# First gate maxima kept one step sooner, one semaphore group for the mLSTM stage, and the feed-forward's first sixteen products in the heads' tail

## What is computed

```python
x = x + tanh(g_xattn[0]) * mlstm(layernorm(x), ctx, ctx, gates, ln_scale)      # 8 heads of 32
x = x + tanh(g_ffn[0])   * ffn(layernorm(x))      # 8-bit weights + rank-16 side path, 256 -> 1024 -> 256
x = x + tanh(g_xattn[1]) * attention(layernorm(x), ctx)                        # 16 heads of 16
x = x + tanh(g_ffn[1])   * experts(layernorm(x))  # 8 routed experts, top 2, and 2 shared
# in mlstm, per head: cs = cumsum(log_sigmoid(f)); m[s] = max over t <= s of (i[t] - cs[t]) (plus cs[s])
#   C = (q k^T / sqrt(32)) * exp(a[t] - m[s]), masked;  h = C v / max(|sum C|, exp(-max)); then layernorm
# in ffn: h = gelu(W z + b + 2 B (A z)), the same form for the way down
```

## Time and profile before

| | |
|---|---|
| median of 3 runs | 1222.02 us (1220.18 to 1222.48) |
| profiled execution | 1218.74 us |
| its span | 1217.1 us |
| mean granted TensorE clock | 0.954 |
| busy: PE, DVE, ACT, POOL | 1117.4, 885.1, 702.3, 420.2 us |

### The profile page before, as it was taken

The page is one execution under the profiler, slowest core; times in us unless marked ns, Lnnn a source line. Parts: engine busy times, 40 slices in busy tenths (PEclk is TensorE's granted clock), DMA queues, the critical chain, the costliest instruction groups (busy, mean ns, idle before and its releaser), DMA issues. The chain is left out here.

```text
span 1217.1 us, 28139 instructions
## 1 busy us (share of the span) xinstructions
PE 1117.4 (92%) x9260; PEld 946.3 (78%) x9261; DVE 885.1 (73%) x2032; ACT 702.3 (58%) x1585; POOL 420.2 (35%) x559
## 2 busy tenths in 40 slices
PE   4869997999998899999998889879999999998997
PEld 1336665888887677777776489869999999998997
DVE  5858996766676788888888377467766776764666
ACT  1378995556572566667666543346755555554543
POOL 1237895531212011111120026663222232223664
PEclk9879999999998899999999878889999999999999
DMA  9246651000005455354453047656455555544664
GB/s 320 79 167 237 226 193 54 1 0 0 0 0 113 98 119 116 87 108 107 89 107 56 2 169 266 219 203 239 166 167 169 165 161 166 164 139 157 190 206 150
DMA packets 97574, 163.51 MB, mean 134 GB/s; under 512 B 12048, under 2 KB 72228, under 8 KB 95172
## 3 DMA queue, kind: packets, MB, share of 16 engines
q1 hardware_dynamic: 87652, 135.05, 38.1%
q0 software_dynamic: 9104, 26.49, 6.2%
q10 hardware_dynamic: 720, 0.71, 0.2%
HBM read 102.47 MB, written 33.69 MB: 112 GB/s over the span
## 5 line engine op out<-in xcount | busy, mean ns | idle before, releaser
L1796 DVE TENSOR_REDUCE c_mx<-d_bank 128x2 f32<-128x512 f32 x256 | 164.4, 686 | 16.5 <-PE d_bank L1948 16.1
L1711 ACT ACTIVATE c_probs<-c_t 128x512 f32<-128x512 f32 x248 | 134.7, 598 | 26.8 <-PE c_t L1974 25.9
L2929 ACT ACTIVATE d_g_full<-d_bank,d_e_bias 128x256 f32<-128x256 f32 x156 | 77.8, 498 | 105.3 <-PE d_bank L34 105.3
L32 PE MATMUL d_bank<-de_zt_hi,d_e_hi 128*128 128x256 f32 x312 | 91.0, 292 | 0.1
L34 PE MATMUL d_bank<-d_w_hi,d_g_lo 128*128 x312 | 87.8, 281 | 0.0
L33 PE MATMUL d_bank<-de_zt_lo,d_e_hi 128*128 128x256 f32 x312 | 87.8, 281 | 0.0
L33 PE MATMUL d_bank<-d_w_lo,d_g_hi 128*128 x312 | 87.8, 281 | 0.0
L32 PE MATMUL d_bank<-d_w_hi,d_g_hi 128*128 x312 | 87.8, 281 | 0.0
L34 PE MATMUL d_bank<-de_zt_hi,d_e_lo 128*128 128x256 f32 x312 | 87.3, 280 | 0.0
L3089 POOL DMA_INDIRECT d_w_lo<-d_y_rows,d_pos x64 | 65.4, 1021 | 53.3 <-ACT d_g_hi L3102 20.6
L1644 POOL CAST c_ct_hi<-c_c_raw 128x512 fp32r<-128x512 f32 x15 | 9.2, 610 | 212.3 <-PE c_misc L34 212.3
(11 more groups left out here) (433 smaller groups left out, 3849.0 us busy)
## 6 DMA issues: line engine op xcount, KB each, us to landing
d_e_raw<-in_w SPq DMA_DIRECT2D x39, 514.0 KB, 3.7
a_mb<-a_maxima SPq DMA_DIRECT2D x16, 1024.0 KB, 7.5
d_w_hi<-d_zt_kept SPq DMA_DIRECT2D x26, 512.0 KB
d_y_rows<-de_ys SPq DMA_DIRECT2D x39, 256.0 KB, 2.1
d_z_in<-d_z_rows POOLq DMA_DIRECT2D x37, 256.0 KB, 4.4
c_kt<-c_k_hi SPq DMA_DIRECT2D x64, 128.0 KB, 3.1
c_qt<-c_q_hi SPq DMA_DIRECT2D x64, 128.0 KB, 3.8
d_zt_kept<-d_w_hi SPq DMA_DIRECT2D x20, 256.0 KB
```

The costliest lines, as they stand in the source:

```text
L32: tensor.matmul(out, lhs_hi, rhs_hi, start=start, stop=False)
L1711: act.activation(probs[h % PR][:], t_bank(n, p, k), ACT.Exp).then_inc(exp_done, 1)
L1796: dve.tensor_reduce(mx[n % 2][:, :, k, p:p + 1], s_ps[h % SB], AX.X, ALU.max).then_inc(max_done, 1)
L2929: act.activation(g_full[:, m, :], hid[m][:, 0:TOK], ACT.Gelu, bias=bias[u][:, m:m + 1]).then_inc(gelu_full, 1)
```

## The change

It has three parts.

1. `rows.keep_maxima(sync, 0)` stands before the placing of the rows of step 6 instead of behind it.
2. The groups `ar_` and `ah_` are gone: `FirstInputs`, `GateRows` and the heads draw from one group `a_`, made ahead of the gates. After the heads one group is cleared, with one barrier, in place of three. The heads' tile `hz` becomes `rows.gates`, which holds `f` and `gate_i`.
3. The four PSUM banks `qk` of the heads and `hid` and `turned` of the feed-forward become one tensor, `lora.banks`, and `low` a tile that lives through both. `lower(0)` and the twelve products of `base(0, 0..2)` run at the end of the heads, behind `turn_outputs`, and so do the ACT and DVE halves of the split of `low`. PE waits for its own last product there. In the feed-forward, PE starts with the three `raised` products, and ACT with a GELU on one column (`primed`), which puts the table load ahead.

```diff
@@ mlstm_gates, sync
             for n in range(STEPS):
                 if n + KR < STEPS:
                     load_kt(n + KR)
+                if n == PLACED - 1:
+                    rows.keep_maxima(sync, 0)
                 if n < PLACED:
                     sync.wait_ge(rows_done, n + 1)
                     place_rows(sync, n)
-            rows.keep_maxima(sync, 0)
             sync.wait_ge(rows.m_kept[0], 16)
             first.load_maxima(sync)
@@ phase_mlstm
-        first = FirstInputs(nc, ctx, ctx_in, ctx_t, ln_scale, lora.ln_s, m_dram)
-        rows = GateRows(nc, ctx, tok_all, ident, m_dram)
+        sem = cleared_semaphores(nc, ctx, "a_")
+        first = FirstInputs(nc, ctx, sem, ctx_in, ctx_t, ln_scale, lora.ln_s, m_dram)
+        rows = GateRows(nc, ctx, sem, tok_all, ident, m_dram)
@@ LoraWeights.hold_zt
+        self.low = ctx.enter_context(nc.sbuf_tensor("b_low", [P, 4 * P], F32R, side="right"))
+        self.banks = self.ctx.enter_context(nc.psum_tensor("b_banks", [P, self.BANKS, 512], F32))
@@ mlstm_heads
-        sem = cleared_semaphores(nc, ctx, "a_")
-        hz = sb("hz", [P, J, D])
-        qk = ctx.enter_context(nc.psum_tensor("a_qk", [P, QUAD, 512], F32))
+        hz = rows.gates
+        qk = lora.banks
@@ heads, scalar
                 keep_outputs(B - 1, g)
+            act.wait_ge(b_low_done, 1)
+            act.activation(lora.low[:], qk[:, LOW, :], ACT.Copy).then_inc(b_low_hi_done, 1)
@@ heads, vector
             normalise(B - 1)
+            dve.wait_ge(b_low_hi_done, 1)
+            pair = slice(lora.G, 2 * lora.G)
+            dve.tensor_tensor(lora.low[pair, :], qk[pair, LOW, :], lora.low[pair, :], ALU.subtract).then_inc(b_low_lo_done, 1)
+            dve.wait_ge(b_low_lo_done, 1)
@@ heads, tensor
             turn_outputs(B - 1)
+            pe.wait_ge(b_zt_lo_done, lora.KD)
+            pe.wait_ge(c_done, B * H)
+            lora.lower(pe, qk[:, LOW, :]).then_inc(b_low_done, 1)
+            for m in range(LOW):
+                mm = lora.base(pe, qk[:, m, :], m)
+            mm.then_inc(b_base_done, 1)
+            pe.wait_ge(b_base_done, 1)
@@ feed-forward, scalar
-            round_low(0)
+            act.sem_inc(low_hi_done, 1)
+            act.activation(primed[:], half_neg[:, 0:1], ACT.Gelu).then_inc(primed_done, 1)
             for m in range(KF):
                 gelu(0, m)
@@ feed-forward, vector
+            dve.sem_inc(low_lo_done, 1)
             stat(1)
-            split_low(0)
@@ feed-forward, tensor
             def hidden_first():
-                for m in range(HR):
-                    base(0, m)
-                pe.wait_ge(low_lo_done, 1)
                 for m in range(HR):
                     raised(m)
...
-            lower(0)
+            pe.sem_inc(low_done, 1)
             hidden_first()
```

More of the change, by code:

```diff
@@ L137 @@
     LATE = 2
+    BANKS = 4
     def __init__(self, nc, ctx, w_fc_t, rank):
+        self.ctx = ctx
         def sb(name, shape, dt=F32R):
@@ L159, in hold_zt, with lower, base @@
         self.late_hn = ctx.enter_context(nc.sbuf_tensor("b_late_hn", [P, 2 * self.LATE, self.D], F32, side="right"))
+        self.low = ctx.enter_context(nc.sbuf_tensor("b_low", [P, 4 * P], F32R, side="right"))
+        self.banks = self.ctx.enter_context(nc.psum_tensor("b_banks", [P, self.BANKS, 512], F32))
+    def lower(self, pe, out):
+        for c in range(self.KD):
+            for part in (self.zt_hi, self.zt_lo):
+                mm = pe.matmul(out, self.down[:, c, :], part[:, c, :], start=(c == 0 and part is self.zt_hi), stop=(c == self.KD - 1 and part is self.zt_lo))
+        return mm
+    def base(self, pe, out, m):
+        for c in range(self.KD):
+            for part in (self.zt_hi, self.zt_lo):
+                mm = pe.matmul(out, self.w1[:, c, m * P:(m + 1) * P], part[:, c, :], start=(c == 0 and part is self.zt_hi), stop=False)
+        return mm
     def hold_w2(self, nc, ctx):
@@ L602, in _, with mlstm_heads @@
             rows.turn(pe, 0, 0, tok_ps[:, 0])
-def mlstm_heads(nc, x_all, tanh_g, ident, half_neg, ctx_in, ctx_t, qt_all, m_dram, tok_all, rows, lora, first):
+def mlstm_heads(nc, sem, x_all, tanh_g, ident, half_neg, ctx_in, ctx_t, qt_all, m_dram, tok_all, rows, lora, first):
     B, S, D, H, DH, J = Mlstm.B, Mlstm.S, Mlstm.D, Mlstm.H, Mlstm.DH, Mlstm.J
@@ L617, in mlstm_heads @@
     MR = 3
+    LOW = lora.BANKS - 1
     PAIR = 2
@@ L1011, in phase_lora_ffn @@
         zt_hi, zt_lo = lora.zt_hi, lora.zt_lo
-        low = sb("low", [P, TOK], F32R)
+        low = lora.low
         g_full = sb("g_full", [P, GR, TOK])
@@ L1018, in phase_lora_ffn @@
         a_stats, a_mv, a_rstd = sb("a_stats", [P, AT, 6]), sb("a_mv", [P, AT, 2]), sb("a_rstd", [P, AT])
-        hid = [bank(f"hid{i}", [P, TOK]) for i in range(HR)]
-        turned = bank("turned", [P, TOK])
+        hid = [lora.banks[:, i, :] for i in range(HR)]
+        turned = lora.banks[:, HR, :]
         y = [bank(f"y{t}", [P, 512]) for t in range(T)]
+        primed, primed_done = sb("primed", [P, 1]), sem("primed_done")
         stats_done, mv_done = sem("stats_done"), sem("mv_done")
@@ L1347, in lower @@
                 pe.wait_ge(zt_lo_done, n * KD + KD)
-                for c in range(KD):
-                    for part in (zt_hi, zt_lo):
-                        mm = pe.matmul(turned[:], down[:, c, :], part[:, c, :], start=(c == 0 and part is zt_hi), stop=(c == KD - 1 and part is zt_lo))
-                mm.then_inc(low_done, 1)
+                lora.lower(pe, turned).then_inc(low_done, 1)
             def base(n, m):
@@ L1355, in base @@
                     pe.wait_ge(gelu_hi, n * KF + m + 1 - HR)
-                for c in range(KD):
-                    for part in (zt_hi, zt_lo):
-                        pe.matmul(hid[m % HR][:], w1[:, c, m * P:(m + 1) * P], part[:, c, :], start=(c == 0 and part is zt_hi), stop=False)
+                lora.base(pe, hid[m % HR], m)
             def raised(m):
```

13 lines of the change are left out of this document (7 added, 6 removed).

## The result

The changed kernel takes 1218.31 us (median of 20 runs, 1214.06 to 1221.01), the kernel before in the same rounds 1221.99 (20 runs, 1216.59 to 1224.64). The ratio is 0.9969 with a 95% interval of 0.9958 to 0.9979: 3.7 us less, 2.6 to 5.1. The profiled execution took 1216.37 us with a span of 1214.8; that of before had 1218.74 and 1217.1.

The account below looks back on a forecast made before the run. DVE was taken to end the feed-forward's first chunk, TensorE to bound all behind it. 2.0 at the first border plus 3.0 - 2.0 = 1.0 at the second took 1222.02 to 1219.0 us; range 1216.5 to 1221.2.

Parts of the forecast that it names:

- Part 1: End of the gates: the earlier store of the maxima brings load, mask and first `weigh` 2.00 us sooner, all kept.
- Part 2: End of the heads: clearing one semaphore group costs 1.49 us where three cost 2.02, saving 0.53 us.
- The tail's start: Heads to feed-forward: sixteen products of 0.24 us start the feed-forward 1.9 us later, yet the first split comes 3.0 sooner.
- The give-back: First chunk: DVE's splits and `norm` now run beside POOL's additions, copy and `ct_lo`, so 2.0 us are lost again.
- TensorE "moves along": First chunk: TensorE's work ends 0.80 us before the second turning; its 40 products start on a DVE result and shift too.
- From the first chunk on: Behind the feed-forward's first chunk TensorE is always busy, so an edit ahead is worth exactly what it moves that point.
- The second border's 1.0: Heads to feed-forward: first split 3.0 us sooner, less 2.0 lost beside POOL, leaves 1.0 us.
- A kept gain: Rival, first chunk: the tail's 3.0 us is kept whole, 5.0 in sum, 1217.0 us; chance 0.20.
- POOL takes it all: Rival, first chunk: each microsecond of POOL's stops DVE, leaving 1.4 us, 1220.6; chance 0.22, including the maxima's store failing.
- The lower clock in the tail: Rival, heads' tail: sixteen products at 1.2 GHz take 0.43 us each, giving 1222.9, up to 1224; chance 0.08.

Follow-up runs that it names:

- part 2 alone: Kernel before, with only the attention's three semaphore groups made one; 1183.20 us, ratio 0.9991.
- `low` alone in the tail: Changed kernel with only the four products for `low` in the heads' tail, the twelve with w1 back in the feed-forward; 1180.12 us, ratio 0.9957.
- POOL's split later: Changed kernel with POOL's `ct_hi` and `ct_lo` moved behind `late_update`; 1180.85 us, ratio 0.9971.
- the kernel before with POOL held back: Kernel before, with POOL's large work held back until DVE's first `zt_lo` of the next chunk; 1191.61 us, ratio 1.0052.
- norm sooner: Changed kernel with DVE's `norm(1)` two splits sooner, POOL unchanged; ratio 0.9984.

## Why the prediction held

The forecast was 3.0 us, 1219.0; measured were 3.7 (1218.31) and, in the rounds of the runs, 3.4. By the marks it is 3.1 to 3.3 at the second turning, which stands 152.18 and 152.10 behind the gates' barrier, before 155.30 and 155.37. Of this 0.3 is lost again: from the second turning to ACT's first table load of the attention it is 155.65 and 155.64, before 155.32 and 155.36. So the traces have 2.8 and 3.0 left there, and the interval of the 3.7 (2.6 to 5.1) takes these in. Step by step:

- **Part 1**, forecast 2.0. From the barrier to T it is 127.3 to 127.6 in six of the eight executions with it and 129.3 to 129.5 in three of the six without; the means of all are 127.1 and 129.1, so 1.9. The load's landing differs by some tenths from one execution to the next (the mask starts 0.1 to 0.6 behind the barrier).
- **Part 2**, forecast 0.53, measured 0.77. The mechanism is right and the size short: I took 1.49 for a border of one group from the gates, and the heads' border with one group is 1.25 behind DVE's last instruction (part 2 alone) and 1.26 (`low` alone in the tail).
- **The tail's start**, forecast: products of 0.24 at the full clock, SP 1.5 behind them, the first split 3.0 sooner. Measured: 0.23 to 0.24, 1.51 and 3.14.
- **The give-back**, forecast 2.0, measured 1.83. The place was right, the split between its terms was not. The two splits met lost 0.1 and 0.3 us, not 0.55 each; `norm(1)` lost 2.2, not 0.46 for two of its four and 1.16 for a third: they took 0.83, 0.90, 0.69 and 1.43 us against 0.40 each (four in 1.37, one overlapping the next). By the Trainium skill, "SBUF — State Buffer", section "Who interferes with whom", whichever of DVE and GpSimd issues first holds their shared pair of ports for its whole instruction while the other blocks, and a DVE instruction with at most one input from SBUF, outside the two-port modes, does not contend; the trace agrees, with 1.43 beside a `ct_lo` of 1.26, and with 0.69 for `zt_lo`, which has one operand in PSUM. That `norm`, with one tile from SBUF, runs in a two-port mode is not shown by any run here. The additions grew too, from 2.82 to 3.79. With the 0.33 that DVE waited for `late_rstds`, and less the 1.16 that the first split no longer lost, that makes 1.8.
- **TensorE "moves along"**: this step failed, without harm to the sum. I had its 0.80 us in hand and did not ask what a late `norm(1)` does to it. It waited 1.88, ran at 0.50 of the clock for some three microseconds and used up the 0.80. With `ct_lo` moved away (POOL's split later) both chains got shorter together, since the wait and the slow clock went with it.
- **From the first chunk on** an edit was to be worth exactly what it moves the second turning. That failed by 0.3 us: a chunk of the changed kernel takes 0.05 more, as told at the end. The second border's 1.0 was hit because 1.31 at the turning and this 0.33 cancelled down to it, which is luck.
- **The rivals.** A kept gain (1217.0) is excluded by `norm` at 3.60 (by the time alone, whose interval goes to 5.1 us, it would not be), and that POOL takes it all (1220.6) by the 1.3 us left at the second turning. The lower clock in the tail did not come: 1.00 from 194 to 204, also in 202 to 204, where the earlier trace rows had 0.50; it came later, behind the wait for `norm(1)`, and cost the 0.80 in hand.

What the whole of part 3 is worth by itself at the second turning is 1.31 - 0.77 = 0.54 us, for sixteen moved products and a table load, and only 0.2 behind the chunks that follow; with the twelve w1 products left where they were it would be 1.5 and 1.2.

## What to carry to other kernels

When an engine is made to start sooner, list what the others do in the stretch that it moves into, and price the meeting instruction by instruction: here 3.1 us became 1.3 because DVE's elementwise work slid under GpSimd's. The same list says where to go on: moving GpSimd's work out of the stretch that sets the end gave 3.0 us more on the changed kernel and 1.1 on the old one. When a queue's work is held back, first look for the short instruction at its end that someone waits for: two instructions, 1.4 us together, behind 13 us of other work cost 8.3 us. Read short effects from marks of one trace to the next, not from times whose interval is as wide as the effect.

## What had not been expected of the hardware

From the gates' barrier to T four executions took 0.7 to 1.8 us less than the others of their kind and one took 0.9 more, for no reason in the code. Two windows of the kernel before and of the kernel before with POOL held back (columns as in the earlier trace rows), whose heads are the same:

```profile
94.00:98.00 4.00, 2.25 (x24) 1.72 (x24) 4.00 (x8) 3.71 (x12) 3.47 (x6) 1.00 0.93 342
98.00:102.00 4.00, 3.40 (x32) 2.40 (x32) 1.75 (x7) 1.85 (x7) 4.00 (x6) 0.67 0.77 289
```

```profile
94.00:98.00 4.00, 1.92 (x24) 1.42 (x18) 4.00 (x9) 3.55 (x12) 3.84 (x6) 1.00 0.93 354
98.00:102.00 4.00, 3.75 (x48) 2.70 (x48) 2.64 (x7) 3.24 (x11) 4.00 (x6) 1.00 0.79 317
```

TensorE is busy for about half of 94 to 98 us in both. In the first the granted clock falls to 0.67 behind it, in the second it stays at 1.00, and 48 products are done in place of 32; from the barrier to T it is 129.29 against 127.50. The 13th of the 64 `weigh` stands 35.00 and 33.09 behind the barrier, and from there to T the two take 94.29 and 94.41, so all of it arises here. Of the fourteen traces three have 1.00 from 98 to 102, this one, norm sooner and `low` alone; they are the three that are 1.1 to 1.8 short. The other eleven have 0.57 to 0.78. So the clock goes with a difference of up to 2 us from one execution to the next, as large as each part of this change. What makes it fall in one execution and not in another was not tried.

The same kernel before takes 1222 us in the rounds of the result and 1185 in those of the runs (1184.95 to 1185.16, on two chips), 3% less, at a mean granted clock of 0.954 and 0.961 in its two traces. The traces show where it lies: up to ACT's first table load of the routed experts' step they take 705.9 and 709.2 us, and from there to the end 511.2 and 474.6. The clock of the first stages has no part in it; whether the chip has, and what slows the last step, is open.

From chunk 2 on, a chunk takes 20.66 us in all eight traces of kernels with the shared tensor of banks, and 20.61 in the six without it; over the layer 0.3 us. The same products are issued; what costs the 0.05 was not tried.
